# Experts of a mixture layer: three sums in DRAM instead of two, and TensorE's 128 tiles written out with one load of the weight place each

## The chip, the cores and the metric

One core of one Trainium2 chip. The metric is the time of the whole program on the device, in microseconds (us). A core has TensorE (matrix products; "PE" in the profile, its weight loads "PEld"), VectorE (DVE), ScalarE (ACT), GpSimd (POOL), SyncE (SP) and 16 DMA engines.

## The reference

Four layers of cross attention and feed-forward on x of 16 x 128 rows of 256 numbers, in float32. What is changed here is the feed-forward part of the second layer, a mixture of 32 experts, of which each row takes 6:

```
scores = softmax(x2d @ wg_router.T);  topk_w, topk_idx = top_k(scores, 6);  topk_w /= sum(topk_w)
g = einsum('ecd,edf->ecf', xe, w_gate)          # xe: the rows of expert e
u = einsum('ecd,edf->ecf', xe, w_up)
ye = einsum('ecf,efd->ecd', silu(g) * u, w_down)
y = sum over the 6 experts of a row of (ye of that row * topk_w)
return y + shared_expert(x2d)
```

x is 2048 x 256, an expert has width 176. The layer adds the result to x, and the third layer's cross attention begins with a layer norm of the sum.

## The kernel before

Every stage of the program is a block in which each engine has its own list of instructions, written out by hand; engines wait for each other through semaphores (`wait_ge`). Nothing but these lists and waits sets the order.

**The experts' loop.** A routing step has put the rows into `slot_x` in DRAM, sorted by expert and padded to tiles of 128 rows: 2048 x 6 / 128 + 32 = 128 tiles (`SLOT_TILES`). A tile has one expert; which, and in which of 8 places in `places` (SBUF) that expert's weights lie, is known only at run time, so the place is read from a table (`router.place`) into a register. Buffers of a tile (`x_in`, `y`, `to`, `share`) form a ring of 8 (`RING`). For tile i the engines do:

- SP: `fetch_weights` (skipped by a condition when the expert is the same as before) and `fetch_rows`, both up to eight tiles ahead; each waits until tile i - 8 has let go of its buffers.
- TensorE, at step i: `expert_up(i)` (4 matmul records in the profile, the gate and up products), `turn_expert(i - 1)` (2), `turn_input(i + 1)` (2), `expert_down(i - 2)` (4).
- ScalarE: silu of the gate, a copy of the turned rows, and `store`, which scales the result by each row's share into `y`.
- VectorE: `move_hidden`, `mark` (target rows `to` and share; it waits until the scatter of tile i - 8 has landed, since that reads `to`) and `multiply_expert`.
- GpSimd: one indirect DMA per tile that adds the 128 rows of `y` to rows of a sum in DRAM (`expert_sums`). Adding is a read and a later write, so two such DMAs on one sum must not overlap. There are `SUMS` = 2 sums, tiles take them in turn, and tile i waits until tile i - 2 has landed. The first sum starts as x plus the shared expert, the other as zeros, written in the first stage by `load_behind`.

TensorE's list is 8 tiles written out, then a loop (`Fori`) of 14 turns with 8 tiles each, then 8 tiles. In the loop a register must not live past the turn, so the first two steps of each turn load two places: that of the tile ahead (i + 1) and once more that of tile i - 2 for `expert_down`, and the first step also that of its own tile i. The other engines but GpSimd have loops of the same form and keep them.

**After the loop.** TensorE computes values (`L1847`) and keys (`L1838`) of the next layer, VectorE and ScalarE take them off. When all scatters have landed, SP reads the sums back in four groups of four row tiles (`L1691`): the first into `x`, the second into `second`, a part of `places`. Of each group VectorE adds `second` to x for two tiles (`L2010`) and GpSimd for the other two (`L1718`); VectorE takes the statistics of the layer norm (`L2014`) of all four, GpSimd the root, ScalarE the norm. The last instruction of this stage is VectorE's `L2103`, after which the next stage (`L2242`) begins.

Of the kernel before, what the change touches and what calls it, by code (L numbers as in the profile page):

```python
# [9 lines left out]
ALU = mybir.AluOpType  # L10
# [863 lines left out]
SHARE_AT = H + 1  # L874
INDEX_AT = SHARE_AT + TOPK
XW = INDEX_AT + TOPK
SUMS = 2
GROUP = 4
GROUPS = B // GROUP
SCATTERS = 3  # L880
# [645 lines left out]
def moe(nc, mem, A, router, norm):  # L1526
# [7 lines left out]
    with ctx:  # L1534
# [47 lines left out]
        gate, up = ([bank(f"{x}{j}") for j in range(2)] for x in ("gate", "up"))  # L1582
        turned, down, pairs, scores = bank("turned"), bank("down"), bank("pairs"), bank("scores")
        both, turned_x, turned_h, down_e = gate, up, turned, [down, pairs]
        second = places[:, 0:B * H].rearrange("p (t n) -> p t n", t=B)

        router.pairs, router.scores = pairs, scores
        down_s = [down, turned]
# [32 lines left out]
        read = [signal(f"read{g}") for g in range(GROUPS)]  # L1621
        stat = signal("stat")
        summed_up, counted_up = signal("summed_up"), signal("counted_up")

        qa, gf, tf = mem.qa, mem.gf, mem.tf
        wkv = part(A["L2_xattn_wkv"])
# [9 lines left out]
        with nc.Block() as block:  # L1636
            @block.sync
            def _(sp):
# [48 lines left out]
                for j in range(RING):  # L1687
                    sp.wait_ge(stored[j].sem, 16 * (SLOT_TILES // RING))
                for g in range(GROUPS):
                    for a, target in enumerate((mem.x, second)):  # L1690
                        sp.dma_start(target[:, g * GROUP:(g + 1) * GROUP, :],  # L1691
                                     mem.sums[a][g * GROUP * P:(g + 1) * GROUP * P, :].rearrange("(t p) h -> p t h", p=P)).then_inc(read[g].sem, 16)

            @block.gpsimd
            def _(pool):
                pool.memset(h_e[:, :, FE:], 0.0).then_inc(ready.sem, 1)
                for t in range(EARLY_ROWS, B):
                    router.scatter(pool, t)
                for j in range(SCATTERS):
                    pool.wait_ge(mem.scattered[j].sem, 16 * TOPK * len(range(j, B, SCATTERS)))  # L1700
                pool.wait_ge(x_stored.sem, 16 * B)
                pool.memset(mem.values[:, :], 1.0).then_inc(ones_set.sem, 1)

                for i in range(SLOT_TILES):
                    j = i % RING
                    pool.wait_ge(y_moved.sem, y_moved.at(i))
                    if i >= SUMS:
                        pool.wait_ge(stored[(i - SUMS) % RING].sem, 16 * ((i - SUMS) // RING + 1))
                    pool.indirect_dma_start(out=mem.sums[j % SUMS], out_offset=bass.IndirectOffsetOnAxis(ap=to[:, j:j + 1], axis=0),  # L1709
                                            in_=y[:, j, :], in_offset=None, bounds_check=T + P - 1, oob_is_err=True,  # L1710
                                            compute_op=ALU.add).then_inc(stored[j].sem, 16)

                for j in range(RING):
                    pool.wait_ge(stored[j].sem, 16 * (SLOT_TILES // RING))
                for t in range(B):
                    if t % GROUP >= 2:
                        pool.wait_ge(read[t // GROUP].sem, 16 * SUMS)
                        pool.tensor_tensor(mem.x[:, t, :], mem.x[:, t, :], second[:, t, :], ALU.add).then_inc(summed_up.sem, 1)  # L1718
                    if t % GROUP == GROUP - 1 and t < B - 1:
                        norm.root(pool, t // GROUP, t - GROUP + 1, t + 1)  # L1720

            @block.tensor
            def _(pe):
# [75 lines left out]
                    last.then_inc(downed_e.sem, 1)  # L1799


                def step(t, j, places, first=False, final=False):
                    i = t * RING + j
                    if j == 0:
                        places[0] = place_of(i)
                    expert_up(i, j, t, places[j])
                    if j < RING - 1:
                        places[j + 1] = place_of(i + 1)
                    if j < 2 and not first:
                        places[j - 2] = place_of(i - 2)  # L1810
                    if not (first and j < 1):
                        turn_expert(i - 1, (j - 1) % RING)
                    if not (final and j == RING - 1):
                        turn_input(i + 1, (j + 1) % RING, t if j < RING - 1 else t + 1)
                    if not (first and j < 2):
                        expert_down(i - 2, (j - 2) % RING, places[j - 2])

                turn_input(0, 0, 0)
                places = {}
                for j in range(RING):  # L1820
                    step(0, j, places, first=True)
                with pe.Fori(1, SLOT_TILES // RING - 1) as t:
                    places = {}
                    for j in range(RING):
                        step(t, j, places)
                places = {}
                for j in range(RING):
                    step(SLOT_TILES // RING - 1, j, places, final=True)
                turn_expert(LAST, LAST % RING)
                expert_down(LAST - 1, (LAST - 1) % RING, places[RING - 2])  # L1830
                expert_down(LAST, LAST % RING, places[RING - 1])

                def keys(n, m):
                    i = n * HC + m
# [88 lines left out]
            def _(dve):  # L1923
# [81 lines left out]
                for t in range(B):  # L2005
# [1 line left out]
                    if t % GROUP == 0:  # L2007
                        dve.wait_ge(read[t // GROUP].sem, 16 * SUMS)
                    if t % GROUP < 2:
                        dve.tensor_tensor(row, row, second[:, t, :], ALU.add).then_inc(counted_up.sem, 1)  # L2010
                        dve.wait_ge(counted_up.sem, counted_up.at(2 * (t // GROUP) + t % GROUP))
                    else:
                        dve.wait_ge(summed_up.sem, summed_up.at(2 * (t // GROUP) + t % GROUP - 2))
# [2077 lines left out]
```

## Time and profile before

| what | value |
|---|---|
| median of 3 runs | 2070.43 us (2069.07 to 2079.79) |
| profiled execution, span | 2074.5 us |
| granted clock of TensorE, mean | 0.960 |
| busy: PE, PEld, DVE, ACT, POOL | 89%, 60%, 61%, 50%, 35% |
| experts' loop, from the first to the last tile's gate product | 977.8 to 1325.5 us |
| reading back the sums until the next stage's first product | 1342.4 to 1368.4 us |

The span is that of the one execution that was profiled, and the times of the rows count from its start. Busy shares are means over stages with different limits; the two stretches in the last lines are the ones that the change touches.

### The profile page before, as it was taken

How to read it: one execution, taken by the hardware profiler on the slowest of the kernel's cores; microseconds unless marked ns; L12 is line 12 of the kernel's file. 1: busy time of each engine (PE TensorE's matmuls, PEld its weight loads, DVE VectorE, ACT ScalarE, POOL GpSimd, SP SyncE). 2: the span in 40 equal slices, each digit the busy share in tenths (PEclk: the TensorE clock that was granted, in tenths of full speed). 3: DMA queues.
4: the chain of work that ended last, by engine and by line, in shares of the span. 5: the costliest groups of instructions: out<-in, count | busy, mean ns of one | idle time of the engine just before them, and what ended most of it. 6: DMA issues, size and time to landing. Idle time of an engine off the chain costs nothing. (4 is left out here: it accounts for less than half of the span.)

```text
span 2074.5 us, 42486 instructions
## 1 busy us (share of the span) xinstructions
PE 1853.4 (89%) x12207; PEld 1251.6 (60%) x12216; DVE 1266.8 (61%) x4137; ACT 1026.9 (50%) x2698; POOL 730.7 (35%) x707
## 2 busy tenths in 40 slices
PE   7999999998999888878999989969978799999755
PEld 4677777775565566545666766735545557777533
DVE  6666666665777344656343334368979545656698
ACT  5555555553333443312444434348879524444586
POOL 3333333331000202566455555533300106676410
PEclk9999999999999898979999999989999898999998
DMA  8990000000000000253777776510010111211100
GB/s 305 283 274 1 0 0 0 0 1 0 0 0 0 1 1 33 76 197 120 170 162 169 169 155 136 92 59 2 2 64 1 64 43 26 42 39 36 43 18 24
DMA packets 145607, 145.55 MB, mean 70 GB/s; under 512 B 49376, under 2 KB 133568, under 8 KB 145344
## 3 DMA queue, kind: packets, MB, share of 16 engines
q1 hardware_dynamic: 122432, 113.81, 19.5%
q0 software_dynamic: 23040, 30.01, 8.2%
q8 instruction: 75, 1.23, 0.2%
q14 instruction: 60, 0.49, 0.1%
HBM read 137.12 MB, written 66.44 MB: 98 GB/s over the span
## 5 line engine op out<-in xcount | busy, mean ns | idle before, releaser
L1709 POOL DMA_INDIRECT expert_sums<-moe_rows_in,moe_to x128 | 198.2, 1549 | 158.7 <-DMA expert_sums<-moe_rows_in,moe_to 91.9
L1782 PE MATMUL moe_gate<-moe_places,moe_xt 128*128 x512 | 175.3, 465 | 3.4 <-issue 1.9
L3329 DVE CUSTOM_DVE_ANT_0 ctxt<-wa_score,early 128x128 f32<-128x128 f32 x512 | 114.2, 286 | 101.3 <-PE wa_score L3179 101.3
L1975 DVE COPY moe_ht_e<-moe_turned 128x256 f32<-128x256 f32 x128 | 54.4, 425 | 193.9 <-PE moe_turned L1790 192.5
L570 ACT ACTIVATE ga_prob<-ga_score,ga_neg_max 128x128 f32<-128x128 f32 x256 | 99.6, 390 | 125.7 <-DVE ga_neg_max L443 125.7
L3141 POOL TENSOR_TENSOR ctxt<-ctxt,wa_top 128x512 f32<-128x512 f32 x128 | 131.6, 1040 | 75.4 <-DVE wa_top L3329 75.4
L2065 POOL TENSOR_TENSOR ln_rstd<-ln_var,half 128x4 f32<-128x4 f32 (+1 forms) x16 | 21.5, 1346 | 362.1 <-DVE ln_var L2061 362.1
L190 POOL TENSOR_TENSOR ga_q_inv<-ga_q_sum,half 128x4 f32<-128x4 f32 x64 | 64.4, 1007 | 224.3 <-DVE ga_q_sum L426 224.3
L3278 ACT ACTIVATE wa_pt<-wa_turned 128x512 f32<-128x512 f32 x128 | 76.5, 598 | 129.7 <-PE wa_turned L3188 129.7
L325 PE MATMUL ga_summed<-ga_wo,ga_out_t 128*128 128x256 f32 x512 | 121.2, 380 | 0.7 <-ACT ga_out_t L578 0.7
L1782 PEld LDWEIGHTS moe_gate<-moe_places,moe_xt 128*128 128x128 f32 x512 | 90.5, 189 | 47.2 <-issue 12.1
L249 PE MATMUL ga_proj<-early,ga_xt 128*128 128x512 f32 x252 | 118.6, 593 | 0.0
L1116 POOL DMA_INDIRECT slot_x<-early x96 | 97.8, 1019 | 56.4 <-issue 27.4
L439 DVE SCALAR_TENSOR_TENSOR ga_score<-ga_scored,ga_q_inv,ga_mask 128x128 f32<-128x128 f32 x256 | 72.2, 344 | 51.6 <-PE ga_scored L297 50.1
L325 PEld LDWEIGHTS ga_summed<-ga_wo,ga_out_t 128*128 128x128 f32 x512 | 92.3, 190 | 11.0 <-ACT ga_out_t L578 1.1
L1889 ACT ACTIVATE moe_act_e<-moe_gate 128x176 f32<-128x176 f32 x128 | 40.6, 317 | 100.0 <-PE moe_gate L1782 99.3
L3179 PE MATMUL wa_score<-wa_keys,wa_qd 32*128 32x128 f32 x1024 | 78.9, 294 | 11.6 <-DVE wa_top L3329 9.0
L3188 PE MATMUL wa_turned<-ident,ctxt 128*128 128x128 f32 x512 | 84.3, 290 | 0.0
L3179 PEld LDWEIGHTS wa_score<-wa_keys,wa_qd 32*128 32x128 f32 x1024 | 66.6, 197 | 26.6 <-issue 23.2
L431 DVE COPY ga_qt<-ga_turned 128x512 f32<-128x512 f32 x63 | 43.5, 690 | 62.5 <-PE ga_turned L289 62.4
L297 PEld LDWEIGHTS ga_scored<-ga_kt,ga_qt 128*128 128x128 f32 x512 | 63.3, 191 | 23.6 <-DVE ga_qt L431 13.9
L556 ACT ACTIVATE ga_square<-ga_q_tok 128x128 f32<-128x128 f32 x256 | 75.0, 294 | 1.3 <-DVE ga_q_tok L394 1.3
(491 smaller groups left out, 4777.6 us busy)
## 6 DMA issues: line engine op xcount, KB each, us to landing
moe_places<-in_L_ffn_packed SPq DMA_DIRECT2D x128, 608.0 KB
slot_x<-zeros SPq DMA_DIRECT2D x24, 1076.0 KB, 16.3
moe_rows_in<-slot_x SPq DMA_DIRECT2D x128, 134.5 KB, 3.0
wa_v<-v_ctx SPq DMA_DIRECT2D x16, 180.0 KB, 3.1
early<-in_L_xattn_Wq SPq DMA_DIRECT2D x5, 512.0 KB, 7.8
x<-in_x SPq DMA_DIRECT2D x4, 512.0 KB, 9.6
ga_wo<-in_L_xattn_Wo SPq DMA_DIRECT2D x1, 2048.0 KB, 15.1
expert_sums<-zeros SPq DMA_DIRECT2D x2, 1024.0 KB, 8.4
```

The lines of the kernel that those rows point to most:

```text
L249: last = pe.matmul(proj[m % 2][:, :], lhs[:, c, :], weight[:, c, :], start=(c == 0), stop=(c == HC - 1))
L325: last = pe.matmul(summed[:, 0:H], out_t[:, h, :], w.wo[:, h, :], start=(h == 0), stop=(h == NH - 1))
L556: last = act.activation(square[:, h, :], q_tok[:, n % 2, h * D:(h + 1) * D], ACT.Square, accum_out=q_sum[:, n % 2, h:h + 1])
L570: last = act.activation(prob[:, n % 2, part], score[:, n % 2, part], ACT.Exp, bias=neg_max[:, n % 2, h:h + 1], accum_out=total[:, n % 2, h ...
L1116: pool.indirect_dma_start(out=self.mem.slot_x, out_offset=bass.IndirectOffsetOnAxis(ap=self.slot_to[:, t, k:k + 1], axis=0), in_=self.mem. ...
L1709: pool.indirect_dma_start(out=mem.sums[j % SUMS], out_offset=bass.IndirectOffsetOnAxis(ap=to[:, j:j + 1], axis=0), in_=y[:, j, :], in_offs ...
L1782: last = pe.matmul(both[j % 2][:, 0:2 * FE], xt[:, j % 2, c, :], packed[:, place, c * 2 * FE:(c + 1) * 2 * FE].rearrange("p a n -> p (a n) ...
L3141: pool.tensor_tensor(unit, unit, top[:, k % LOWS, :].unsqueeze(2).to_broadcast([P, QUAD, P]), ALU.subtract).then_inc(lowered.sem, 1)
L3179: last = pe.matmul(score[(QUAD * u + r) % 3][:, x * P:(x + 1) * P], w.qd[rows, j % 2, QUAD * u + x, :], w.keys[rows, j % 2, QUAD * u + x, ...
L3188: last = pe.transpose(turned[k % 2][:, x * P:(x + 1) * P], low[:, k % LOWS, x, :], mem.ident[:, :])
L3278: act.activation(pt[:, (k // 2) % 2, :, k % 2, :], turned[k % 2][:, :].rearrange("p (x m) -> p x m", x=QUAD), ACT.Exp).then_inc(pt_moved.s ...
L3329: ins = dve.tensor_tensor_reduce(unit[:, x, :], score[k % 3][:, x * P:(x + 1) * P], w.table[:, k, x, :], 1.0, NEVER, ALU.add, ALU.max, top ...
```

## The change

`SUMS` becomes 3. The scatter of tile i goes to sum i mod 3 and waits for tile i - 3. The third sum is zeroed in the first stage like the second (three more DMAs, two of them of 1 MB and one of 128 KB), read back into `third` (another part of `places`), and added to x by an instruction of its own behind that of `second`, on the same engine, with a wait between the two. TensorE's three parts become one list of 128 steps; the place of tile i + 1 is loaded in step i behind `expert_up(i)`, once, and stays in its register until `expert_down(i + 1)`.

```diff
-SUMS = 2
+SUMS = 3
...
-        second = places[:, 0:B * H].rearrange("p (t n) -> p t n", t=B)
+        second, third = (places[:, k * B * H:(k + 1) * B * H].rearrange("p (t n) -> p t n", t=B) for k in range(SUMS - 1))
...
-                    for a, target in enumerate((mem.x, second)):
+                    for a, target in enumerate((mem.x, second, third)):
...
-                    pool.indirect_dma_start(out=mem.sums[j % SUMS], out_offset=bass.IndirectOffsetOnAxis(ap=to[:, j:j + 1], axis=0),
+                    pool.indirect_dma_start(out=mem.sums[i % SUMS], out_offset=bass.IndirectOffsetOnAxis(ap=to[:, j:j + 1], axis=0),
...
-                        pool.tensor_tensor(mem.x[:, t, :], mem.x[:, t, :], second[:, t, :], ALU.add).then_inc(summed_up.sem, 1)
+                        pool.tensor_tensor(mem.x[:, t, :], mem.x[:, t, :], second[:, t, :], ALU.add).then_inc(summed_two.sem, 1)
+                        pool.wait_ge(summed_two.sem, summed_two.at(2 * (t // GROUP) + t % GROUP - 2))
+                        pool.tensor_tensor(mem.x[:, t, :], mem.x[:, t, :], third[:, t, :], ALU.add).then_inc(summed_up.sem, 1)
...
-                def step(t, j, places, first=False, final=False):
-                    i = t * RING + j
-                    if j == 0:
-                        places[0] = place_of(i)
-                    expert_up(i, j, t, places[j])
-                    if j < RING - 1:
-                        places[j + 1] = place_of(i + 1)
-                    if j < 2 and not first:
-                        places[j - 2] = place_of(i - 2)
...
-                with pe.Fori(1, SLOT_TILES // RING - 1) as t:
-                    places = {}
-                    for j in range(RING):
-                        step(t, j, places)
...
+                turn_input(0, 0, 0)
+                place = {0: place_of(0)}
+                for i in range(SLOT_TILES):
+                    t, j = divmod(i, RING)
+                    expert_up(i, j, t, place[i])
+                    if i < LAST:
+                        place[i + 1] = place_of(i + 1)
+                    if i >= 1:
                         turn_expert(i - 1, (j - 1) % RING)
-                    if not (final and j == RING - 1):
-                        turn_input(i + 1, (j + 1) % RING, t if j < RING - 1 else t + 1)
-                    if not (first and j < 2):
-                        expert_down(i - 2, (j - 2) % RING, places[j - 2])
+                    if i < LAST:
+                        turn_input(i + 1, (j + 1) % RING, (i + 1) // RING)
+                    if i >= 2:
+                        expert_down(i - 2, (j - 2) % RING, place.pop(i - 2))
...
-                        dve.tensor_tensor(row, row, second[:, t, :], ALU.add).then_inc(counted_up.sem, 1)
+                        dve.tensor_tensor(row, row, second[:, t, :], ALU.add).then_inc(counted_two.sem, 1)
+                        dve.wait_ge(counted_two.sem, counted_two.at(2 * (t // GROUP) + t % GROUP))
+                        dve.tensor_tensor(row, row, third[:, t, :], ALU.add).then_inc(counted_up.sem, 1)
```

TensorE's list before, at the end of a turn of the loop and the first step of the next (`L1797` expert_down, `L1822` the loop's branch, `L1775` loads of a place, `L1782` expert_up, `L1790` turn_expert):

```order
664 L1797 ISA
665 L1797 MATMUL moe_pairs<-moe_places,moe_ht_e 128x256
666 L1822 REGISTER_ALU
667 L1822 COMPARE_AND_BRANCH
668 L1775 TENSOR_LOAD early
669 L1775 ISA x2
670 L1782 ISA
671 L1782 MATMUL moe_gate<-moe_places,moe_xt 128x352
672 L1782 ISA
673 L1782 MATMUL moe_gate<-moe_places,moe_xt 128x352
674 L1775 TENSOR_LOAD early
675 L1775 ISA x2
676 L1775 TENSOR_LOAD early
677 L1775 ISA x2
678 L1790 MATMUL moe_turned<-ident,moe_h_e 128x128 x2
```

The branch, the load ahead of the gate product and the second of the two loads behind it are what only the first steps of a turn have.

The same list of the changed kernel, from one step into the next (the lines have moved by three: `L1800` expert_down, `L1785` expert_up, `L1778` the load, `L1793` turn_expert, `L1774` turn_input):

```order
568 L1800 MATMUL moe_pairs<-moe_places,moe_ht_e 128x256
569 L1785 ISA
570 L1785 MATMUL moe_gate<-moe_places,moe_xt 128x352
571 L1785 ISA
572 L1785 MATMUL moe_gate<-moe_places,moe_xt 128x352
573 L1778 TENSOR_LOAD early
574 L1778 ISA x2
575 L1793 MATMUL moe_turned<-ident,moe_h_e 128x128 x2
576 L1774 MATMUL moe_up<-ident,moe_rows_in 128x128 x2
```

Every step has these rows now, with one load behind the gate product.

## Rows read from the trace of the kernel before

**Rows 1.** Busy time by stretch: us, busy (records) of each engine, granted clock, DMA share, GB/s.
```profile
1000.00:1240.00 240.00, 227.93 (x1064) 162.52 (x1062) 95.62 (x442) 104.54 (x267) 131.62 (x85) 1.00 0.78 167
```

**Rows 2.** TensorE's timeline at the start of a turn: start, duration, what, [idle before].
```profile
1109.78 1.45 PE L1782 MATMUL moe_gate<-moe_places,moe_xt 128*128 x4
1111.78 0.41 PE L1790 MATMUL moe_turned<-ident,moe_h_e 128*128 128x128 f32 x2 [0.55 <-issue]
...
1113.11 1.38 PE L1782 MATMUL moe_gate<-moe_places,moe_xt 128*128 x4
...
1116.13 1.35 PE L1782 MATMUL moe_gate<-moe_places,moe_xt 128*128 x4
...
1123.59 1.35 PE L1782 MATMUL moe_gate<-moe_places,moe_xt 128*128 x4
```

**Rows 3.** TensorE's loads of a place: durations in ns, min/median/max.
```profile
L1775 PEldq FUSED_REGOPS  x284: 46/151/168, 976.0 to 1323.6; - x142
L1775 PEldq TENSOR_LOAD <-early x158: 296/302/704, 975.3 to 1323.2; - x158
```

**Rows 4.** TensorE's timeline: gate products of tile 3 and of tile 127.
```profile
990.61 1.35 PE L1782 MATMUL moe_gate<-moe_places,moe_xt 128*128 x4
...
1325.51 1.36 PE L1782 MATMUL moe_gate<-moe_places,moe_xt 128*128 x4
```

**Rows 5.** Who waited for whom, 1000 to 1330 us: total, times, longest.
```profile
POOL expert_sums L1709 <- DMA expert_sums<-moe_rows_in,moe_to: 88.6, 51, 3.7
...
DVE moe_to L1981 <- DMA expert_sums<-moe_rows_in,moe_to: 10.4, 12, 2.1
```

**Rows 6.** GpSimd's timeline: a scatter, and the next but one with its idle time.
```profile
1242.50 1.55 POOL L1709 DMA_INDIRECT expert_sums<-moe_rows_in,moe_to  x1 [0.31 <-issue]
...
1249.52 1.54 POOL L1709 DMA_INDIRECT expert_sums<-moe_rows_in,moe_to  x1 [2.62 <-DMA expert_sums<-moe_rows_in,moe_to]
```

**Rows 7.** VectorE's and TensorE's timelines where a scatter is late.
```profile
1239.92 0.15 DVE L1981 COPY moe_to<-moe_rows_in 128x1 uint32<-128x1 uint32 x1 [2.13 <-DMA expert_sums<-moe_rows_in,moe_to]
...
1238.16 1.35 PE L1782 MATMUL moe_gate<-moe_places,moe_xt 128*128 x4
...
1242.95 0.85 PE L1782 MATMUL moe_gate<-moe_places,moe_xt 128*128 x2 [0.60 <-DVE moe_h_e L1970]
```

**Rows 8.** The scatters' time from issue to landing.
```profile
DMA to landing us min/median/max: 3.6/4.0/6.8
```

**Rows 9.** Timeline behind the loop: product, last scatter, first read, VectorE, GpSimd, next stage.
```profile
1330.37 13.98 PE L1847 MATMUL moe_gate<-qa_wv,ctxt 128*128 128x256 f32 x64
...
1338.46 1.54 POOL L1709 DMA_INDIRECT expert_sums<-moe_rows_in,moe_to  x1 [0.32 <-issue]
...
1342.37 0.39 SPq L1691 DMA_DIRECT2D x<-expert_sums  x1
...
1344.39 0.69 DVE L2002 TENSOR_TENSOR early<-moe_gate,qa_bv 128x512 f32<-128x512 f32 x1 [1.03 <-PE moe_gate L1847]
...
1349.45 0.42 DVE L2010 TENSOR_TENSOR x<-x,moe_places 128x256 f32<-128x256 f32 x1 [4.37 <-DMA moe_places<-expert_sums]
1349.59 1.74 POOL L1718 TENSOR_TENSOR x<-x,moe_places 128x256 f32<-128x256 f32 x2 [9.59 <-DMA moe_places<-expert_sums]
...
1366.31 1.13 DVE L2103 TENSOR_SCALAR early<-early,x_step 128x256 f32<-128x256 f32 x4
1368.42 1.57 PEld L2242 LDWEIGHTS qa_turned<-ident,early 128*128 128x128 f32 x8 [8.13 <-DVE early L2103]
```

**Rows 10.** The zeroing in the first stage: duration of an issue in ns, first and last start.
```profile
L3903 SPq DMA_DIRECT2D expert_sums<-zeros x4: 486/1937/3797, 143.8 to 148.8; - x4
```

**Rows 11.** DMA queue that brings instructions, and busy time by stretch, 1750 to 1850/1950 us.
```profile
q8 instruction: 26, 0.43, 0.9%
...
1750.00:1850.00 100.00, 93.42 (x1623) 75.15 (x1614) 61.03 (x482) 48.87 (x90) 69.16 (x68) 1.00 0.20 42
```

**Rows 12.** SP's own wait for free weight buffers, 970 to 1345 us.
```profile
SPq L1660 <- PE moe_pairs L1797: 23.0, 37, 1.9
```

More of the change, by code:

```diff
@@ L1623, in moe @@
         summed_up, counted_up = signal("summed_up"), signal("counted_up")
+        summed_two, counted_two = signal("summed_two"), signal("counted_two")
         qa, gf, tf = mem.qa, mem.gf, mem.tf
@@ L1799, in expert_down @@
                     last.then_inc(downed_e.sem, 1)
-                def step(t, j, places, first=False, final=False):
-                    i = t * RING + j
-                    if j == 0:
-                        places[0] = place_of(i)
-                    expert_up(i, j, t, places[j])
-                    if j < RING - 1:
-                        places[j + 1] = place_of(i + 1)
-                    if j < 2 and not first:
-                        places[j - 2] = place_of(i - 2)
-                    if not (first and j < 1):
-                        turn_expert(i - 1, (j - 1) % RING)
-                    if not (final and j == RING - 1):
-                        turn_input(i + 1, (j + 1) % RING, t if j < RING - 1 else t + 1)
-                    if not (first and j < 2):
-                        expert_down(i - 2, (j - 2) % RING, places[j - 2])
-                turn_input(0, 0, 0)
-                places = {}
-                for j in range(RING):
-                    step(0, j, places, first=True)
-                with pe.Fori(1, SLOT_TILES // RING - 1) as t:
-                    places = {}
-                    for j in range(RING):
-                        step(t, j, places)
-                places = {}
-                for j in range(RING):
-                    step(SLOT_TILES // RING - 1, j, places, final=True)
+                turn_input(0, 0, 0)
[6 more added lines that the diff above has]
+                    if i >= 1:
+                        turn_expert(i - 1, (j - 1) % RING)
+                    if i < LAST:
+                        turn_input(i + 1, (j + 1) % RING, (i + 1) // RING)
+                    if i >= 2:
+                        expert_down(i - 2, (j - 2) % RING, place.pop(i - 2))
                 turn_expert(LAST, LAST % RING)
-                expert_down(LAST - 1, (LAST - 1) % RING, places[RING - 2])
-                expert_down(LAST, LAST % RING, places[RING - 1])
+                expert_down(LAST - 1, (LAST - 1) % RING, place.pop(LAST - 1))
+                expert_down(LAST, LAST % RING, place.pop(LAST))
                 def keys(n, m):
```

## The prediction

> **What bounds the kernel now.** I read the busy time by stretch first. In the experts' loop TensorE is busy 227.93 of 240 us at full clock, every other engine far less, and the DMA engines 0.78 of the time [rows 1]. So the loop goes at TensorE's pace, and the question is where its list runs slower than its products need. The timeline of TensorE answers it. Inside a turn three tiles take 1123.59 - 1116.13 = 7.46 us, 2.487 each, with no idle time: the products lie end to end. The first tile of a turn takes 1113.11 - 1109.78 = 3.33 us and the second 1116.13 - 1113.11 = 3.02, with TensorE idle for nothing that another engine did ("issue", 0.55 us before the turn of the hidden rows) [rows 2]. From tile 3 to tile 127, 124 tiles take 1325.51 - 990.61 = 334.9 us [rows 4]; at 2.487 they would take 308.4. The loop has **26.5 us** above its products.
>
> The waits name a second holder. GpSimd's scatters wait 88.6 us for earlier scatters to land, 51 times, and VectorE's `mark`, which needs the scatter of eight tiles ago, waits 10.4 us in 12 cases [rows 5]. Where such a wait is longest, tile 95 takes 1242.95 - 1238.16 = 4.79 us instead of 2.49: VectorE starts 2.13 us late, and TensorE waits for it [rows 7]. So two sums are already a little too slow for TensorE at its present pace, and the ring of eight tiles takes up most of it.
>
> **Taking the places once.** A load of a place is a register load of 302 ns (median; 296 to 704) and 151 + 46 ns of register work behind and before it [rows 3]: about 0.5 us on TensorE's own queue, in which nothing behind it starts. The loads are now 158, and will be 128; the 30 that go are the second ones in the first two steps of a turn, at 15 places (14 turns and the closing part), and with them the 14 branches and the load ahead of a turn's first product, which moves behind the product of the step before, where each other step has its own. One turn's end costs 3.33 + 3.02 - 2 x 2.487 = 1.38 us [rows 2]. An extra load in the second step costs 3.02 - 2.487 = 0.53 us, as much as the load itself, so one load beside the gate product (1.35 us of matmul) hides just, and a second is paid in full. That is the reason to expect a written-out step to be like a step inside a turn, and no faster. 15 x 1.38 = **20.7 us** off. The loops of ScalarE, VectorE and SP stay; their branches fall into idle time of these engines, and cost nothing while it is there (their longest part would be about 0.2 us a turn, 3 us over 15 turns, if the cover went).
>
> **Three sums.** What is left of the excess, 26.5 - 20.7 = 5.8 us, is in part late scatters (2.3 us in the tile of [rows 7] alone, the rest in shorter ones) and in part loads of the slow kind, up to 704 ns [rows 3], which stay. I take 5.0 of it as recovered, with 2.3 and 5.8 as the ends. This holds only if three sums are fast enough for 2.49 us a tile. With two, a scatter starts at the earliest when the last but one has landed; in the backlog that was as much as 1249.52 - 1242.50 = 7.02 us later, of which 2.62 us idle [rows 6]; landing takes 3.6 to 6.8 us, 4.0 in the median [rows 8]. From landing to the next start there pass a few tenths more. With three sums and a tile each 2.49 us, a scatter may take 3 x 2.49 = 7.5 us from its start to that of the third behind it, more than the slowest landing with its few tenths; and GpSimd's own part is 1.55 + 0.31 us a tile [rows 6]. So the scatters would be bound by their rows, not by each other. With two sums the limit at this pace would be 5.0 us, less than the slow ones take: most of what TensorE's list saves would then go into waits for scatters.
>
> **Behind the loop.** TensorE leaves the experts at 1330.4 (E, below) and goes on with 13.98 us of values. The last scatter starts at 1338.46, 8.1 us behind E, since a backlog is left; the reads start at 1342.37, VectorE's additions at 1349.45 = E + 19.1 [rows 9]. After: with no backlog the last scatter starts about 1 us behind E (the scaling into `y` and a few tenths, an estimate), lands 4 us later, and the reads start at about E + 5.1 instead of E + 12.0. But VectorE has its eight additions of values first, until 1344.39 + 0.69 = E + 14.7 [rows 9], and the first group is now three reads instead of two: 7.1 us before (1349.45 - 1342.37), about 9 now (by half the bytes more, less the first transfers' start), so E + 14.1. Additions start at E + 14.9 instead of E + 19.1: 4.2 us gained. Against it stand the 16 new additions: eight on VectorE of 0.42 us, and eight on GpSimd of 0.87 [rows 9] (1.74 for two). Per group VectorE gets 0.9 us more of its own; where GpSimd is the later one (two rows, now four additions, up to 3.5 us, behind the root of the group before) it is up to 1.4. Four groups at 0.9 to 1.4: 3.7 to 5.6 us, and I take 5.2, since VectorE waited for GpSimd in this stretch already. Sum of this part: **1.0 us lost**, with -1 and +5 as ends.
>
> **The rest.** The third sum's zeros go behind all other loads of the first stage, whose DMAs of this kind are issued at 143.8 to 148.8 us [rows 10] and are waited for only in the third stage; 2.2 MB more there cost nothing, and would cost some 8 us if someone waited at once. SP's list doesn't change; it waits 23.0 us for TensorE's release of weight buffers under one of the two result tiles' names alone [rows 12], so it is not at its limit. I give 0.5 us for slow loads at places where a branch hid them before.
>
> **Sum.** -20.7 - 5.0 + 1.0 + 0.5 = -24.2 us on the span: 2074.5 to 2050.3. The profiled execution lies 4 us (0.2%) above the median of the runs, so the median goes from 2070.4 to 2046.
>
> **Weighed against the Trainium skill.** The trace has register loads of 302 ns on TensorE's queue, of which one hides [rows 2, 3]. The Trainium skill, DMA: Bandwidth & Descriptors, "Latency and other measured facts", gives a floor of about 600 ns for such a load. By that, 0.3 us more a tile would not hide, 37 us in all, and the loop would be longer than now; the trace disagrees, since a tile with one load takes 2.49 us with no idle time. The rival with the chance 0.01 below is what this rule would do.
>
> **The rivals.**
> - *Written-out steps run late* because each load is only just covered: every 0.1 us that a step's load is slower than now costs 12 us over 124 tiles. For it: loads reach 704 ns. Against: in tiles inside a turn, 90 in number, this is already the state, and they hold 2.49. With 0.1 us a step: 2058. Chance 0.08. With 0.3 us a step, 37 us, it would be 2083; nothing in rows 3 has that in the median, so chance 0.01.
> - *The scatters stay the bound*: three in flight at 0.8 DMA share land later than two. It needs 7 us in the mean, against 4.0 [rows 8]; each 0.1 us a tile costs 12 us. At 2.6 us a tile, and a backlog at the end: 2063. Chance 0.05. If they are as slow as now per tile (about 2.7), nothing changes: 2071; chance 0.02.
> - *The end of the stage costs more*: reads of 6.3 MB instead of 4.2 and additions that hold each other up, 5 us beyond my sum: 2051. Chance 0.08.
> - *The other side: the instructions don't come in time.* TensorE's loop was fetched once and then run 14 times; now its 104 further tiles come from DRAM while the DMA engines are at 0.78. From 1750 to 1950 us, written-out code too, the queue brings 26 packets for about 3,200 matmul and 3,200 load records (1623 and 1614 in the first half) [rows 11]; 104 x 12 matmul records with a few more register instructions make about 15 packets. For a loss of 10 us each would have to stop TensorE (24 + 10) / 15 = 2.3 us. Against: in that stretch TensorE is busy 93 of 100 us with a packet every 7.7 us, over twice as often as in the experts' list (15 in 308 us is one in 20), if at a DMA share of only 0.20. Time: 2081. Chance 0.04. The Trainium skill, Runtime: NRT & Kernel Launch, "Instruction fetch mechanics", says that straight code is fetched ahead in blocks and a block's end is mostly hidden; rows 11 agree.
> - *More than I think*: all 5.8 us of the excess and no loss at the end, -27 us: 2043; within my range.
>
> **How the numbers follow.** My forecast, 2041 to 2050, has 0.72 (the last rival included); the others as given. 2046 is the likeliest. The range for 8 in 10 takes in the worse end of the stage and part of the late steps: 2040 to 2057. A change of under 0.5% (10 us) can't be told from none here. Faster than 2060: 0.72, the costlier end of the stage and the late steps, less a little for a loss that is larger than there said, 0.87; within 10 us: the bound scatters and that little, 0.09; slower: 0.04.
>
> **What would show it.** In the profile after: gate products 2.48 to 2.50 us apart nearly throughout, no "issue" idle beyond the step's own, tile 3 to tile 127 in 308 to 311 us; 128 register loads; no wait of VectorE's `mark` for a scatter; GpSimd waiting for ScalarE's `y`, not for DMA; the last scatter within 2 us of the last `y`; VectorE's additions beginning 14 to 16 us behind the last expert product and the next stage about 39 us behind it (38.0 now). The prediction is wrong if steps of 2.6 us and more appear without a turn's end, if landings rise above 7 us, or if TensorE stops at even distances of some 8 tiles or more for nothing that an engine did.

## The result and the profile after

| | before | changed |
|---|---|---|
| median of 4 runs each | 2069.75 us (2068.96 to 2079.79) | 2051.41 us (2049.9 to 2053.5) |
| ratio, 95% interval | | 0.9905 [0.9885, 0.9926] |
| profiled execution, span | 2074.5 us | 2049.0 us |
| tile 3 to tile 127 | 334.9 us | 312.2 us |
| first product behind the experts (E) to next stage | 38.1 us | 41.2 us |
| first gate product to next stage | 390.6 us | 371.6 us |

The change makes the program 18.3 us faster, 0.9%; 24 had been forecast. The two spans differ by 25.5 us, but 3.5 us of this lie ahead of the experts' first product and 3.0 us behind the stage. But for the third sum's zeros the change touches neither, and over the ten kernels here they vary by far more, 969.5 to 983.3 us ahead and 699.9 to 709.5 us behind. In the stage itself it is 390.6 - 371.6 = 19.0 us, which agrees with the medians. So what follows speaks of this stretch: tile 3 to 127 22.7 us shorter, the first three tiles 0.6 longer (they take 12.2 to 13.6 us in the ten kernels), the part behind E 3.1 longer.

Busy time by stretch, after, as [rows 1]:

```profile
1000.00:1100.00 100.00, 100.00 (x477) 72.54 (x476) 42.57 (x200) 46.67 (x119) 61.60 (x40) 1.00 0.85 178
1100.00:1200.00 100.00, 100.00 (x480) 72.80 (x479) 42.61 (x200) 46.96 (x120) 61.92 (x40) 1.00 0.86 183
```

TensorE is busy all the time now (227.93 of 240 us before), at the same full clock, and the DMA share has risen from 0.78 to 0.85. TensorE's timeline, after, where a turn of the loop began before (ScalarE's loop still has its turn there), and the products of tiles 3 and 127, as [rows 2, 4]:

```profile
987.68 1.90 PE L1785 MATMUL moe_gate<-moe_places,moe_xt 128*128 x4
...
1139.03 1.37 PE L1785 MATMUL moe_gate<-moe_places,moe_xt 128*128 x4
1141.53 1.36 PE L1785 MATMUL moe_gate<-moe_places,moe_xt 128*128 x4
1144.04 1.44 PE L1785 MATMUL moe_gate<-moe_places,moe_xt 128*128 x4
1146.62 1.36 PE L1785 MATMUL moe_gate<-moe_places,moe_xt 128*128 x4
...
1299.86 1.36 PE L1785 MATMUL moe_gate<-moe_places,moe_xt 128*128 x4
```

A tile takes 2.50 us, and once in eight 1146.62 - 1144.04 = 2.58; nothing is left of the 3.33 and 3.02 of a turn's start. But 2.50 isn't the 2.487 of a step inside the old loop. Tile 3 is a case of its own: it takes 990.72 - 987.68 = 3.04 us, since TensorE is at the lower of its two levels, 1.2 GHz (granted clock 0.50), until this tile's products run (from 975 to 984 us it had been busy 4.7 of 9 us, and the clock fell in the last 4 of these):

```profile
986.00:988.00 2.00, 2.00 (x6) 1.64 (x6) 0.83 (x5) 0.45 (x2) 0.00 (x0) 0.50 0.26 69
```

From 990 us on the clock is 1.00. In the kernel before, the clock was back at 0.96 in the 2 us from 990 us, where tile 3 began, and tile 3 took 2.49 us. Who waited for whom from 1000 to 1300 us (total, times, longest), as [rows 5]:

```profile
POOL expert_sums L1710 <- ACT moe_rows_in L1883: 88.2, 90, 2.9
...
POOL expert_sums L1710 <- DMA expert_sums<-moe_rows_in,moe_to: 21.1, 21, 1.3
PEld moe_gate L1785 <- issue: 19.4, 120, 0.2
```

GpSimd waits for ScalarE's `y` now; its waits for a landing are 21.1 us with none over 1.3 (88.6 and 3.7 before), and VectorE's `mark` has none. The last row shows where 2.50 comes from (e3 tests it): every one of the 120 gate products has its weight load 0.16 us late for "issue".

Behind the loop, timeline after, as [rows 9]:

```profile
1303.58 1.55 POOL L1710 DMA_INDIRECT expert_sums<-moe_rows_in,moe_to  x1 [0.74 <-ACT moe_rows_in L1883]
1304.72 3.62 PE L1836 MATMUL moe_gate<-qa_wv,ctxt 128*128 128x256 f32 x16
1305.43 1.55 POOL L1710 DMA_INDIRECT expert_sums<-moe_rows_in,moe_to  x1 [0.30 <-ACT moe_rows_in L1883]
...
1307.29 1.55 POOL L1710 DMA_INDIRECT expert_sums<-moe_rows_in,moe_to  x1 [0.30 <-issue]
...
1311.08 0.39 SPq L1692 DMA_DIRECT2D x<-expert_sums  x1
...
1319.34 0.74 DVE L1999 TENSOR_TENSOR x<-x,moe_places 128x256 f32<-128x256 f32 x1
1319.76 0.91 POOL L1719 TENSOR_TENSOR x<-x,moe_places 128x256 f32<-128x256 f32 x1
1320.12 0.83 DVE L2001 TENSOR_TENSOR x<-x,moe_places 128x256 f32<-128x256 f32 x1
1320.99 0.43 DVE L2005 BATCH_NORM_STATS2 stats<-x 128x6 f32<-128x256 f32 x1
...
1328.81 0.43 DVE L2005 BATCH_NORM_STATS2 stats<-x 128x6 f32<-128x256 f32 x1 [1.06 <-POOL x L1721]
...
1338.00 2.47 DVE L2082 TENSOR_SCALAR early<-early,ln_scale 128x256 f32<-128x256 f32 x4
...
1343.73 1.13 DVE L2094 TENSOR_SCALAR early<-early,x_step 128x256 f32<-128x256 f32 x4
1345.92 1.14 PEld L2233 LDWEIGHTS qa_turned<-ident,early 128*128 128x128 f32 x6 [12.88 <-issue]
```

VectorE adds from E + 14.6 (19.1 before), so 4.5 us earlier. But from its first addition to the end of its last instruction in this stage, called the chain below, it takes 1344.86 - 1319.34 = 25.5 us instead of 18.0. Additions last 0.74 and 0.83 us where they begin beside GpSimd's, four instructions that round (`L2082`, called the roundings) 2.47 together instead of 1.35, and VectorE waits 1.06 us for GpSimd.

### The profile page after: what moved, and what is told of

Its sections match the earlier page's. It is cut to its first block and busy times, and to the rows that moved or that the text cites. A ratio compares the mean times of both kernels' runs of the same rounds, so it can differ in the third digit from the quotient of the medians.

```text
span 2049.0 us, 42097 instructions
## 1 busy us (share of the span) xinstructions
PE 1831.8 (89%) x12207; PEld 1240.5 (61%) x12215; DVE 1270.2 (62%) x4145; ACT 1026.7 (50%) x2698; POOL 737.9 (36%) x715
## 5 line engine op out<-in xcount | busy, mean ns | idle before, releaser
L1785 PE MATMUL moe_gate<-moe_places,moe_xt 128*128 x512 | 177.9, 470 | 1.9 <-issue 1.9
L1785 PEld LDWEIGHTS moe_gate<-moe_places,moe_xt 128*128 128x128 f32 x512 | 87.7, 191 | 50.4 <-issue 23.6
```

The source lines that it names most:

```text
L1785: last = pe.matmul(both[j % 2][:, 0:2 * FE], xt[:, j % 2, c, :], packed[:, place, c * 2 * FE:(c + 1) * 2 * FE].rearrange("p a n -> p (a n) ...
```

## Experiments

Eight kernels. The loop's figures are the distances of gate products in the one profiled execution of each, the chain and what follows it are counted from E, the first product of the values. "Ends" is what the first two tiles of eight, 15 times from tile 8 on, take above 2 x 2.487 us, "rest" what the other tiles from tile 3 on take above 2.487 each. The kernel before ran again beside them: 2068.35 us in the median beside e1 to e4, 2069.09 beside e5 and e6, 2066.68 beside e7 and e8; the ratios are to these. By time e3 to e8 can't be told from the changed kernel unless their intervals lie apart, as that of e4 does; the distances in the traces are steadier (tile 3 to 127 takes 308.73 or 308.74 us in e3, e7 and e8), and the readings rest on them.

| kernel | ratio to before, 95% | tile 3 to 127 | ends | rest | chain | next stage | first gate to next stage |
|---|---|---|---|---|---|---|---|
| before | | 334.9 | 19.6 | 6.9 | 18.0 | E + 38.1 | 390.6 |
| changed | 0.9905 [0.9885, 0.9926] | 312.2 | 1.6 | 2.2 | 25.5 | 41.2 | 371.6 |
| e1 | 1.0030 [0.9998, 1.0062] | 334.1 | 7.1 | 18.7 | 18.1 | 39.7 | 392.3 |
| e2 | 1.0022 [0.9999, 1.0045] | 332.5 | 23.5 | 0.6 | 25.5 | 41.2 | 391.9 |
| e3 | 0.9920 [0.9903, 0.9936] | 308.7 | 0.5 | -0.1 | 25.6 | 41.3 | 367.2 |
| e4 | 0.9985 [0.9967, 1.0003] | 324.2 | 14.1 | 1.8 | 25.5 | 41.2 | 382.8 |
| e5 | 0.9898 [0.9852, 0.9944] | 308.8 | 0.0 | 0.4 | 25.6 | 41.3 | 368.2 |
| e6 | 0.9862 [0.9822, 0.9902] | 311.6 | 1.6 | 1.6 | 19.8 | 35.5 | 364.2 |
| e7 | 0.9883 [0.9846, 0.9921] | 308.7 | 0.5 | -0.1 | 24.1 | 39.7 | 366.8 |
| e8 | 0.9888 [0.9839, 0.9936] | 308.7 | 0.5 | -0.1 | 26.6 | 42.3 | 368.5 |

### e1: the written-out list with two sums

```diff
-SUMS = 3
+SUMS = 2
```

and without the reads and additions of `third`.

> The changed kernel with the sums part taken back: two sums, TensorE's 128 steps written out. My theory: TensorE offers a tile each 2.50 us, but a scatter waits for the last but one to land, and with two sums that gives about 2.7 us a tile while the experts' weights are being fetched. So tile 3 to tile 127 takes 322 to 333 us (312 in the changed kernel, 335 before), VectorE's mark waits for scatters tens of us in total, and the time is 2060 to 2068 us. Rival: the scatters were never a bound and the third sum only adds work behind the loop: tile 3 to tile 127 in 312 us, and the time is 3 us below the changed kernel's, 2048.

Measured: 2073.12 us, no gain, where 2060 to 2068 had been expected; tile 3 to 127 takes 334.1 us, just over the 322 to 333 expected. Waits of e1, 1000 to 1300 us, and its timeline at the tile that starts at 1124.63:

```profile
POOL expert_sums L1710 <- DMA expert_sums<-moe_rows_in,moe_to: 98.5, 53, 3.2
...
DVE moe_to L1968 <- DMA expert_sums<-moe_rows_in,moe_to: 37.7, 37, 2.1
```

```profile
1124.63 1.44 PE L1783 MATMUL moe_gate<-moe_places,moe_xt 128*128 x4
...
1126.26 0.15 DVE L1968 COPY moe_to<-moe_rows_in 128x1 uint32<-128x1 uint32 x1 [2.01 <-DMA expert_sums<-moe_rows_in,moe_to]
1126.82 0.34 DVE L1957 TENSOR_TENSOR moe_h_e<-moe_act_e,moe_gate 128x176 f32<-128x176 f32 x1
...
1127.21 0.44 PE L1791 MATMUL moe_turned<-ident,moe_h_e 128*128 128x128 f32 x2 [1.14 <-DVE moe_h_e L1957]
...
1128.57 1.36 PE L1783 MATMUL moe_gate<-moe_places,moe_xt 128*128 x4
```

The chain of causes is in these rows: a scatter lands late, `mark` waits 2.01 us for it, the product of VectorE behind `mark` is late, TensorE waits 1.14 us for the hidden rows, and the tile takes 3.94 us. `mark` waits 37.7 us in all (10.4 before, in a window 30 us longer). The turns' ends are gone, and the time has gone into the scatters: "rest" is 18.7 us, and late scatters are also in the 7.1 of "ends". In the whole loop 21 tiles take over 2.7 us, all from tile 36 on; they hold 22.7 of the 25.7 us above the products, and in 20 of them TensorE stands idle for VectorE's product. Register loads were slow as well in this run (40 of 128 took over 0.4 us), but 30 of these lie in tiles that are on time, so they are not the cause. Written out alone, the list gains 0.8 us in the loop.

### e2: three sums with the old loop of TensorE

```diff
 with pe.Fori(1, SLOT_TILES // RING - 1) as t:
     places = {}
     for j in range(RING):
         step(t, j, places)
```

stays as before; the rest is that of the changed kernel.

> The kernel before with three sums, TensorE's loop kept. My theory: only the stalls by late scatters go, so tile 3 to tile 127 takes 329 to 330 us (335 before), the ends of turns still cost 1.38 us each; behind the loop the backlog of scatters is gone but the reads and additions cost more, net 3 us lost; time 2066 to 2069 us. Rival: the scatters are most of the loss and the list's form matters little: tile 3 to tile 127 in under 320 us, 2056 us or less.

Measured: 2073.78 us, where 2066 to 2069 had been expected, and tile 3 to 127 in 332.5 us instead of 329 to 330. TensorE's timeline at a turn of e2:

```profile
1138.79 1.45 PE L1785 MATMUL moe_gate<-moe_places,moe_xt 128*128 x4
1141.07 0.41 PE L1793 MATMUL moe_turned<-ident,moe_h_e 128*128 128x128 f32 x2 [0.84 <-issue]
...
1142.40 1.38 PE L1785 MATMUL moe_gate<-moe_places,moe_xt 128*128 x4
...
1145.51 1.35 PE L1785 MATMUL moe_gate<-moe_places,moe_xt 128*128 x4
```

The late tiles are gone ("rest" 0.6 instead of 6.9), so three sums do what was said of them. But this turn's end costs 1145.51 - 1138.79 - 4.97 = 1.75 us, and all 15 together 23.5 instead of 19.6, so that the loop gains 2.4 us, and the third sum's additions take it back. Neither half is worth anything alone: 0.8 and 2.4 us in the loop, against 22.7 together. Together with e1 this says that the turns' ends had been the pause in which two sums caught up.

### e3: the wait for the turned rows first

```diff
 def expert_up(i, j, t, place):
-    pe.wait_ge(fetched[j].sem, t * 16 + 16)
     pe.wait_ge(xt_moved.sem, xt_moved.at(i))
+    pe.wait_ge(fetched[j].sem, t * 16 + 16)
     pe.wait_ge(multiplied_e.sem, multiplied_e.at(i, -2))
```

> The changed kernel; in expert_up the wait for the moved input stands ahead of the wait for the weights, which leaves it as the wait of the register instruction itself instead of a separate wait ahead of it. My theory for the step of 2.503 us instead of 2.486: the separate wait lets the register instruction and the second weight load start 0.05 to 0.1 us later, so the second gate product starts 0.018 us late; with the order turned round the step is 2.486 to 2.490 and tile 4 to tile 127 takes about 307 us instead of 309.1; time 2049. Rival: the step is longer since the DMA engines are busier (0.86 instead of 0.78) or for another cause, and nothing moves.

Measured: 2049.71 us, and steps of 2.487. Its ratio, 0.9920, is no better than the changed kernel's, so its gain shows in the distances alone. The instructions that TensorE's queue runs for these waits (ns, min/median/max), first of the changed kernel, then of e3:

```profile
L1783 PEldq EVENT_SEMAPHORE  x128: 806/932/2260, 972.1 to 1298.7; - x128
```

```profile
L1783 PEldq EVENT_SEMAPHORE  x128: 51/51/51, 967.4 to 1289.3; - x128
```

and e3's waits in the view of before:

```profile
PEld moe_gate L1785 <- issue: 2.2, 13, 0.2
```

In the trace each step has one separate instruction for these waits, and behind it the register instruction that forms the weights' address. A wait that rides on the latter leaves no row, so which wait stands where is argued from the code's order and these durations: the first in the code rides, the others are in the separate one. Written out, `fetched` came first, and `xt_moved`, the one that comes last in time, was in the separate one (932 ns of waiting), with the register instruction still to run behind it. Now the separate one passes at once, and the late wait is the last thing before the product. In the loop of the kernel before the separate one passed at once too, while in the 16 tiles outside the loop it waited 410 to 1366 ns (ns, min/median/max of all):

```profile
L1780 PEldq EVENT_SEMAPHORE  x114: 51/51/1366, 976.3 to 1324.5; - x114
```

Tile 3 to 127: 308.7 us, 3.5 less. Of this, 0.55 us is tile 3, which is the clock's and not the waits': e5 has this order too and 3.03 us for tile 3, and e6 has the changed kernel's order and 2.51. From tile 4 on the order of the waits is worth 309.1 - 306.2 = 2.9 us (2.1 expected).

### e4: written out, with the loop's loads put back

```diff
 t, j = divmod(i, RING)
+if j == 0 and i:
+    place[i] = place_of(i)
 expert_up(i, j, t, place[i])
 if i < LAST:
     place[i + 1] = place_of(i + 1)
+if j < 2 and i >= RING:
+    place[i - 2] = place_of(i - 2)
```

> The changed kernel, written out, but with the loads of the loop: at each eighth tile a load of its own place ahead of its gate product and one more for the tile two back, at the tile behind it one more for the tile two back. My theory: the loads are what a turn's end cost (1.38 us), not the loop's branch, so at each of the 15 places 1.1 to 1.4 us come back and the time is 2066 to 2072 less the branch's share, 2067 to 2070. Rival: the branch and the loop's register work cost most of it: under 0.5 us at each place, 2056 us or less.

Measured: 2063.39 us, less than expected (2067 to 2070); its ratio of 0.9985 isn't told from the kernel before, so the split is read from the distances. TensorE's timeline of e4:

```profile
1126.74 1.40 PE L1785 MATMUL moe_gate<-moe_places,moe_xt 128*128 x4
...
1129.57 1.44 PE L1785 MATMUL moe_gate<-moe_places,moe_xt 128*128 x4
...
1132.84 1.35 PE L1785 MATMUL moe_gate<-moe_places,moe_xt 128*128 x4
```

These two tiles take 2.83 and 3.27 us; the 15 pairs lose 14.1 us, against 23.5 with the loop (e2) and 1.6 in the changed kernel. So the loads, here one more per turn than the loop had, are 12.5 of 21.9 us, somewhat under 60%. The other 9.4 us, 0.6 a turn, go with the loop's form: the branch and the register work of a turn, but in part also loads that were slower in e2 (24 of 158 over 0.4 us, 13 of 173 in e4), about 3 us by their durations. The prediction had not split this, and its sum doesn't need it; a writer who only removes loads would get a little over half.

### e5: ScalarE written out too

```diff
-with act.Fori(1, SLOT_TILES // RING - 1) as t:
+for t in range(1, SLOT_TILES // RING - 1):
```

on top of e3.

> The changed kernel with the wait order of the third experiment and ScalarE's 128 steps written out as well. My theory: the 0.08 us that TensorE still loses once in eight tiles is ScalarE's turn, in whose first step a register instruction stands between the wait for the gate product and the silu; written out it goes, 15 x 0.08 = 1.2 us, and no tile from 8 on takes over 2.50 us; time 2048. Rival: it is VectorE's or SP's turn, and one tile in eight stays at 2.56 or more.

Measured: 2051.63 us. Two products of e3 where ScalarE's turn lies, then the same stretch of e5:

```profile
1136.17 1.38 PE L1785 MATMUL moe_gate<-moe_places,moe_xt 128*128 x4
1138.69 1.35 PE L1785 MATMUL moe_gate<-moe_places,moe_xt 128*128 x4
```

```profile
1137.02 1.35 PE L1785 MATMUL moe_gate<-moe_places,moe_xt 128*128 x4
1139.51 1.35 PE L1785 MATMUL moe_gate<-moe_places,moe_xt 128*128 x4
```

The step of 2.52 becomes 2.49, so the slow eighth step was ScalarE's turn. It is worth 0.5 us in the loop, not the 1.2 expected, since e3's order had already brought it from 0.08 to 0.03 us a turn; no median here can show either.

### e6: without the third sum's additions

```diff
-dve.tensor_tensor(row, row, third[:, t, :], ALU.add).then_inc(counted_up.sem, 1)
+dve.sem_inc(counted_up.sem, 1)
```

and the same on GpSimd.

> The changed kernel without the 16 additions of the third sum (its part of the experts' result is missing from the output); the reads stay. My theory: the additions, and what VectorE and GpSimd lose by working beside each other, are the 7.5 us by which the chain from VectorE's first addition to its last instruction of the stage has grown (18.0 to 25.5 us), so that chain takes 18 to 19.5 us here and the time is 2044 to 2046. Rival: the third sum's reads make the later groups late, and the chain stays above 22 us.

Measured: 2044.00 us, chain 19.8. Without the 16 additions the chain is 5.7 us shorter. The 1.8 of the 7.5 that stay are the rival's: VectorE now waits for reads at the start of the second and of the third group, 1.95 us in all, which the changed kernel never does in its chain:

```profile
1322.69 0.43 DVE L1999 TENSOR_TENSOR x<-x,moe_places 128x256 f32<-128x256 f32 x1 [0.89 <-DMA moe_places<-expert_sums]
...
1327.19 0.43 DVE L1999 TENSOR_TENSOR x<-x,moe_places 128x256 f32<-128x256 f32 x1 [1.06 <-DMA moe_places<-expert_sums]
```

So the additions hide the third sum's reads, and taking them out uncovers these.

### e7: GpSimd's root behind its next additions

```diff
-if t % GROUP == GROUP - 1 and t < B - 1:
-    norm.root(pool, t // GROUP, t - GROUP + 1, t + 1)
+if t % GROUP == GROUP - 1 and t > GROUP:
+    norm.root(pool, t // GROUP - 1, t - 2 * GROUP + 1, t - GROUP + 1)
```

> The kernel of e3 (the wait for the turned rows first) with one more change: GpSimd does its four additions of group g + 1 ahead of the root of group g, not behind it. Computes the whole reference. In the changed kernel VectorE waits 1.06 + 0.16 us for GpSimd's additions in the second and in the third group each. Theory A (part of the loss behind the loop is GpSimd's place of the root: it stands idle 2.8 us ahead of it and is late behind it): these 2.4 us go, though some additions now lie beside VectorE's; VectorE's chain from its first addition to its last instruction 23 to 24 us instead of 25.6, the next stage 39 to 40 us behind the last expert product instead of 41.3; time 2047 to 2049. Rival B (the two engines slow each other by so much that the waits only turn into longer instructions): 25 to 26 us, next stage at 41. Rival C (the reads of 6.3 MB set the pace of the groups): VectorE then waits for a DMA at the start of a group, and the chain stays over 25.

Measured: 2045.85 us, chain 24.1 and next stage at E + 39.7; theory A gave 23 to 24 for the chain, 39 to 40 for the next stage and 2047 to 2049. Waits of the changed kernel from 1318 to 1346 us, then of e7:

```profile
POOL ln_rstd L2056 <- DVE ln_var L2052: 5.5, 3, 2.8
...
DVE stats L2005 <- POOL x L1721: 2.4, 4, 1.1
```

```profile
POOL ln_rstd L2056 <- DVE ln_var L2052: 0.4, 1, 0.4
```

VectorE's 2.4 us of waits for GpSimd are gone, and the four roundings take 1.14 us instead of 2.47, since GpSimd's additions are over by then. Of these 3.7 us only 1.5 are gained. The rest is what rival B said: other instructions of VectorE now lie beside GpSimd's additions, and six on no more than 128 x 4 numbers take 0.59 to 0.70 us instead of 0.16, as this one:

```profile
1327.14 0.69 DVE L2052 SCALAR_TENSOR_TENSOR ln_var<-ln_diff,ln_var 128x4 f32<-128x4 f32 x1
```

### e8: all additions on VectorE

```diff
-if t % GROUP < 2:
-    ...
-else:
-    dve.wait_ge(summed_up.sem, ...)
+dve.tensor_tensor(row, row, second[:, t, :], ALU.add).then_inc(counted_two.sem, 1)
+dve.wait_ge(counted_two.sem, counted_two.at(t))
+dve.tensor_tensor(row, row, third[:, t, :], ALU.add).then_inc(counted_up.sem, 1)
+dve.wait_ge(counted_up.sem, counted_up.at(t))
```

> The kernel of e3 with all 32 additions of the sums on VectorE and none on GpSimd, which keeps the roots. Computes the whole reference. Measures what an addition costs VectorE with nothing beside it. Theory A (beside GpSimd's additions some of VectorE's instructions take 0.74 to 0.83 us instead of 0.42, and four roundings 2.47 instead of 1.35): now every addition takes 0.41 to 0.43 us and the four roundings 1.35; 16 more additions at 0.45 are +7.2 us, the waits for GpSimd that go -2.4, the slow instructions that go about -3.5: chain 26 to 27.5 us, next stage at 42 to 43. Rival B (the long durations come from the reads that land at the same time, or from the instruction itself): the durations of 0.74 to 0.83 us stay in the first groups, and the chain is 29 us or more.

Measured: 2048.00 us, chain 26.6. VectorE's additions (ns, min/median/max), of the changed kernel and then of e8:

```profile
L1999 DVE TENSOR_TENSOR x<-x,moe_places x8: 407/413/744, 1319.3 to 1341.6; 128x256 f32<-128x256 f32 x8
...
L2001 DVE TENSOR_TENSOR x<-x,moe_places x8: 424/424/834, 1320.1 to 1342.1; 128x256 f32<-128x256 f32 x8
```

```profile
L1992 DVE TENSOR_TENSOR x<-x,moe_places x16: 407/408/418, 1318.6 to 1342.7; 128x256 f32<-128x256 f32 x16
...
L1994 DVE TENSOR_TENSOR x<-x,moe_places x16: 424/425/426, 1319.1 to 1343.1; 128x256 f32<-128x256 f32 x16
```

With nothing of GpSimd beside them all 32 additions take 0.41 to 0.43 us while the same reads land, and the four roundings 1.14 in e8's timeline (2.47 in the changed kernel's). The long ones were GpSimd's doing, and rival B falls. The chain is nevertheless 1 us longer than e3's, for VectorE has 16 additions more.

## Why the prediction was right, and where it was off

**What bounds the kernel** was right: the loop lost 22.7 us with no product changed, and TensorE is at 100 of 100 us.

**Turn ends, 20.7 us.** Held. The same code with three sums, as a loop and written out, gives 332.5 and 312.2 us (e2 and changed), 20.3; the pairs at the turns' starts alone give 23.5 - 1.6 = 21.9. From the kernel before itself the same pairs give less, 19.6 - 1.6 = 18.0: the one turn that was read cost 1.38 us, the mean of the 15 is 1.31, and 1.6 us stay at these places. The reason given, a second load paid in full, explains a little over half (e4).

**Late scatters, 5.0 us.** Held: all tiles outside the turns' starts had 6.9 us of excess, of which three sums leave 0.6 (e2) and the changed kernel 2.2, for the other reasons below; 4.7 us were gained there. That "most of what TensorE's list saves would then go into waits" with two sums is what e1 shows, to the full. The rival of scatters that stay the bound falls: issue to landing is 3.5/4.1/6.8 us (min/median/max) after, [rows 8] before.

**"A written-out step like a step inside a turn" is the first step that failed.** The order of instructions looked the same in both, but not which wait stands in the separate instruction. 2.503 instead of 2.487 us over 108 tiles is 1.7 us, and e3, which changes nothing but the order of two waits, takes 2.9 off the tiles from 4 on. The trace of the kernel before held the answer, for its last eight tiles stand outside the loop. Their products come 2.50 and 2.51 us apart, not 2.487, with the same separate wait in front of them:

```profile
1318.00 1.36 PE L1782 MATMUL moe_gate<-moe_places,moe_xt 128*128 x4
1320.50 1.37 PE L1782 MATMUL moe_gate<-moe_places,moe_xt 128*128 x4
1323.01 1.36 PE L1782 MATMUL moe_gate<-moe_places,moe_xt 128*128 x4
```

"Branches fall into idle time, and cost nothing" was off by ScalarE's part, 0.08 us a turn (1.2 us in 15), 0.03 with e3's order (e5). Tile 3 adds 0.55 us by its clock, which is chance here. The 0.5 us for slow loads weren't needed: counted in the traces, 18 of 158 loads took over 0.4 us before, 1 of 128 now. So the loop came out 2.5 us above its forecast, 312.2 instead of 309.7.

**Behind the loop, 1.0 us lost, is the second.** 3.1 were. The gain was right (4.2 foreseen, 4.5 found), and for the reason given: the additions wait for VectorE's values, not for reads. That the reads are in by then is in part two errors that cancel: they start at E + 6.4 instead of E + 5.1, since the last scatter, said to come at E + 1, came at E + 2.6 (the last three `y` come closer together than GpSimd's 1.86 us a scatter), and the first group takes 7.2 us instead of 9 (GpSimd's first addition, which waits for the reads alone, starts at E + 13.6). The term mis-sized is the additions, 5.2 against 7.5 us. Of the 7.5, eight additions at 0.45 us apart are 3.6; waits for GpSimd 2.4 instead of 0.40 + 0.25 + 0.36 + 0.26 = 1.3 before, 1.1 more; instructions lengthened beside GpSimd 0.32 + 0.41 + 0.41 + 0.41 on four additions, and 2.47 - 1.35 on the roundings, together 2.7. The sum had priced a VectorE addition at the 0.42 us of [rows 9] wherever it lay. The Trainium skill, SBUF — State Buffer, "SBUF: two separate sides", says that a VectorE instruction with two inputs in SBUF and a GpSimd one that reads SBUF lock each other out. The runs agree: additions (two inputs) double, the statistics (one input) keep 0.43 us beside GpSimd, and in e7 even instructions with two inputs of 128 x 4 numbers last about 0.5 us longer. The roundings have one tensor as input and lengthen all the same; the section names a two-port mode of VectorE as a second case, and no run here shows whether they use it.

**The sum.** With -22.7 + 0.6 + 3.1 = -19.0 us in the stage instead of -24.2, 2051.4 lies 5.4 us above the likeliest value. It is inside the range for 8 in 10, 2040 to 2057, but above the 2041 to 2050 that had the chance 0.72. The missing 5.2 us are 2.5 in the loop, 2.1 behind it and 0.6 in the first three tiles. That the profiled span, 2049.0, lies so close to the 2050.3 of the sum is luck: 6.5 us of its fall lie outside the stage.

**The other rivals.** Instructions that come late: no step over 2.6 us from tile 4 on, at a DMA share of 0.86, so the written-out list is supplied in time. The queue that brings instructions has 17 packets from 1000 to 1300 us, 2 before, so the 15 foreseen did come and cost nothing that shows. The rival of late steps was right that steps are longer, by 0.016 us instead of 0.1, but not for its reason: the loads are no slower (301 ns in the median, 302 before), and what moved the step back was the order of the waits. The costlier end of the stage named the time, 2051, and its reason, additions that hold each other up, is borne out by e8; but it is 2.1 us beyond the sum and not 5, and the loop supplied the rest.

**The best kernel** is e7: its stage takes 366.8 us, 4.8 less than the changed kernel's and 23.8 less than before. Its ratio of 0.9883 [0.9846, 0.9921] overlaps with 0.9905 [0.9885, 0.9926], so by time alone it isn't told from the changed one.

**Open.** Why the 15 turns' ends cost 23.5 us with three sums and 19.6 with two is not settled; register loads are slower there (24 of 158 over 0.4 us instead of 18), which is 2 us of the 3.9. Nor is which mode makes the roundings longer beside GpSimd.

## What to carry to other kernels

Two limits that lie close together must be lifted together: each change alone showed nothing (e1, e2), the pair 0.9%, so a part that "does nothing" is not to be dropped before its partner was tried. Where several waits guard one product, put the one that ends last where it stays on the last instruction before the product, and look in the trace at which queue instruction waits. A trace that holds both forms of a step, in and outside a loop, prices them against each other before anything is changed. Work split between VectorE and GpSimd is to be priced with both running, and GpSimd's next independent work goes ahead of what it must wait for.

## What was not expected of the hardware

- The order of the waits ahead of one product has a price: 0.016 us a step, when the separate wait instruction takes 932 ns in the median instead of 51, with a register instruction behind it (changed kernel against e3).
- A VectorE addition of 128 x 256 numbers takes 0.41 to 0.43 us alone and 0.83 beside GpSimd's, and four roundings 1.14 and 2.47; GpSimd's own go from 0.72 to as much as 0.97. It isn't the size that counts: instructions of 128 x 4 numbers go from 0.16 to 0.70 (e7).
- A loop's turn costs TensorE 0.4 to 0.6 us even without its extra loads (e2 against e4).
